# A small read moved up ScalarE's transfer queue, and four bias matmuls moved into the leading tile's x product

## The reference, cut to what matters

```python
h  = x @ W.T + b + ((x @ A[slot]) @ B[slot]) * 2.0        # per batch row of 128 tokens: its own adapter
z  = h @ base_w.T + base_b                                # the second layer
r  = h @ A2.T                                             # 64 hidden columns
p  = softmax(h @ router_w.T)                              # 16 experts
topw, topi = top_k(p, 2); topw = topw / (sum(topw) + 1e-6)
out = x + z + 0.5 * einsum(combine(topw, topi), r, experts)
```

## Time and profile before

| | us |
|---|---|
| runs shown: median of 3 (lowest, highest) | 102.35 (102.18, 102.44) |
| the profiled execution | 102.43 |
| its span in the profile | 100.0 |
| TensorE busy | 96.1 |
| VectorE, ScalarE, GpSimd busy | 66.5, 41.4, 22.3 |
| mean DMA rate over the span | 169 GB/s |

### The profile page before, as it was taken

How to read it: one execution, slowest core, us unless ns; L and a number is a source line. 1 busy time by engine, 2 the same in 40 slices (tenths; PEclk the granted TensorE clock), 3 DMA queues, 4 the chain that set the end, 5 groups by cost and what they waited for, 6 DMA issues and landing times.

```text
span 100.0 us, 1809 instructions
## 1 busy us (share of the span) xinstructions
PE 96.1 (96%) x572; PEld 87.1 (87%) x572; DVE 66.5 (67%) x184; ACT 41.4 (41%) x101; POOL 22.3 (22%) x34
## 2 busy tenths in 40 slices
PE   6899999999999999999999999999999999999990
PEld 6798999999999999998898899878777877878980
DVE  5639997998384884999978567357949275572101
ACT  1705545968778446656531610461334022040000
POOL 4100003234999974208213000000000000000000
PEclk9999999999999999999999999999999999999999
DMA  2999569999958446291970928216228164020211
GB/s 34 370 366 375 179 128 370 290 410 436 328 111 161 158 133 154 61 214 33 239 236 11 253 76 206 108 33 193 99 86 248 29 195 120 0 105 0 105 52 52
DMA packets 8154, 16.90 MB, mean 169 GB/s; under 512 B 1539, under 2 KB 3971, under 8 KB 8018
## 3 DMA queue, kind: packets, MB, share of 16 engines
q1 hardware_dynamic: 7474, 16.41, 53.8%
q10 hardware_dynamic: 640, 0.40, 1.3%
q0 software_dynamic: 32, 0.00, 0.0%
HBM read 13.28 MB, written 2.16 MB: 154 GB/s over the span
## 4 chain that ended last, share of the span: by engine, by line
PE 89%; DMA 6%; DVE 1%; SPq 1%; issue 0%
PE pair L815 86%; DMA w_raw_all<-w_cat 6%; PE pair L957 1%; PE pair L959 1%; PE pair L977 1%; SPq L267 1%; DVE w_hi_all L614 0%; DVE xn L809 0%; PE pair L934 0%; PE pair L947 0%; PE pair L936 0%; PE pair L926 0%
## 5 line engine op out<-in xcount | busy, mean ns | idle before, releaser
L815 PE MATMUL pair<-e_hi,w_hi_all 128*128 128x512 f32 (+1 forms) x72 | 27.1, 376 | 0.0
L815 PE MATMUL pair<-e_hi,w_lo_all 128*128 128x512 f32 (+1 forms) x72 | 26.7, 370 | 0.0
L815 PE MATMUL pair<-e_lo,w_hi_all 128*128 128x512 f32 (+1 forms) x72 | 26.6, 370 | 0.0
L530 ACT ACTIVATE w_hi_all<-exp_raw_all 128x512 fp32r<-128x512 f32 x16 | 9.7, 630 | 15.3 <-DVE exp_raw_all L750 15.3
L815 PEld LDWEIGHTS pair<-e_hi,w_lo_all 128*128 128x128 f32 x72 | 13.5, 188 | 2.5
L815 PEld LDWEIGHTS pair<-e_hi,w_hi_all 128*128 128x128 f32 x72 | 13.5, 188 | 2.5
L815 PEld LDWEIGHTS pair<-e_lo,w_hi_all 128*128 128x128 f32 x72 | 13.6, 189 | 2.0
L757 DVE TENSOR_TENSOR w_lo_all<-exp_raw_all,w_hi_all 128x512 fp32r<-128x512 f32 x16 | 10.4, 689 | 4.5 <-ACT w_hi_all L530 3.9
L750 DVE TENSOR_TENSOR exp_raw_all<-w_raw_all 128x512 f32<-128x512 f32 x16 | 11.4, 753 | 0.0
L764 DVE TENSOR_TENSOR xn<-pair,xn 128x512 f32<-128x512 f32 x7 | 4.8, 690 | 8.9 <-PE pair L815 8.9
L815 PE MATMUL pair<-p_hi,x_hi 128*128 128x304 f32 x32 | 9.9, 310 | 0.0
(11 more groups left out here) (107 smaller groups left out, 162.5 us busy)
## 6 DMA issues: line engine op xcount, KB each, us to landing
w_raw_all<-spill SPq DMA_DIRECT2D x16, 256.0 KB, 4.0
exp_raw_all<-experts SPq DMA_DIRECT2D x4, 512.0 KB, 8.6
xn<-x_n SPq DMA_DIRECT2D x4, 512.0 KB, 7.2
out<-xn SPq DMA_DIRECT2D x7, 256.0 KB, 2.0
w_raw_all<-w_cat SPq DMA_DIRECT2D x3, 552.0 KB, 6.8
xt_raw<-x_t SPq DMA_DIRECT2D x2, 512.0 KB, 6.7
xt_raw<-x_t SPq DMA_DIRECT2D x1, 1024.0 KB, 12.6
c_stack<-c_hi SPq DMA_DIRECT2D x7, 74.0 KB, 3.8
```

The lines of the kernel that those rows point to most:

```text
L530: nc.scalar.activation(gt_hi[:, t % 2, js, :], g[:, js, :], ACT.Copy).then_inc(gh_done, 1)
L815: return nc.tensor.matmul(out_ap, lhs, rhs, start=first, stop=last)
```

## The change

On ScalarE's queue the probe goes out between the left and the right piece of the leading block. On TensorE the four bias matmuls go ahead of the last k of x_other(0), instead of behind it.

```diff
@@ ScalarE @@
-            for n, cols in enumerate((W_LEFT, W_RIGHT)):
-                act.dma_start(w_raw[:, 0, cols], w_cat[0, :, cols]).then_inc(in_w_side[n], 16)
+            act.dma_start(w_raw[:, 0, W_LEFT], w_cat[0, :, W_LEFT]).then_inc(in_w_side[0], 16)
             act.dma_start(probe[:, :, :], w_cat[1:KC, 0:P:8, 0:R].rearrange("k p n -> p k n")).then_inc(in_probe, 16)
+            act.dma_start(w_raw[:, 0, W_RIGHT], w_cat[0, :, W_RIGHT]).then_inc(in_w_side[1], 16)
@@ TensorE @@
             def x_other(t):
                 out_cols, cols = other_half[t % 2]
-                x_side(t, out_cols, cols).then_inc(pe_x, 1)
-
-            def x_side(t, out_cols, cols):
+
+                x_side(t, out_cols, cols, bias_within=t == 0).then_inc(pe_x, 1)
+
+            def x_side(t, out_cols, cols, bias_within=False):
                 par = t % 2
                 x_h, x_l = x_his[t % XB], x_los[t % XB]
                 for k in range(KC):
+                    if k == KC - 1 and bias_within:
+                        bias()
                     if t == 0 and k == 0:
                         pe.wait_ge(pl_done, KC)
...
             x_first(0)
             x_other(0)
-            bias()
             lora_first_transpose()
```

## The result

The changed kernel is slower: 104.94 us median of 6 runs (104.59 to 106.36) against 102.39 (102.06 to 103.25), ratio 1.0241 with an interval of 1.0205 to 1.0276. I had forecast 102.20 and a range up to 103.0. The profiled execution took 105.26, its span is 103.5. Some executions of nearly every kernel here are longer than its others by one per cent or more; the medians keep them, the ratios and intervals leave them out, so a median can lie high beside its ratio.

What follows compares the result with a forecast made beforehand. The bound was taken as the moment the k = 1 block can be multiplied, plus fixed TensorE work and holes. From the 102.35 median, 0.15 off for the bias edit and zero for the queue's edit gave 102.20 us, range 101.85 to 103.0.

Steps and rivals of the forecast that it cites:

- The bound: Whole kernel: time is when the k = 1 block can be multiplied, plus fixed TensorE work, plus holes.
- The bias edit: TensorE in x_other(0): bias sums done 0.42 us earlier, no wait for bp_lo, gain 0.15 us.
- the hole of 0.15: TensorE idle 0.15 us ahead of L934's weight load at 27.06, given to L683's bias_rows; the bias edit closes it.
- The queue's edit: ScalarE's queue: right piece issued 0.45 us later, covered on every path; the sum taken as zero.
- The covers: Lateness of the right piece that costs nothing: up to 0.54 us on ScalarE, 0.9 on TensorE's right rows.
- Rival 2: ScalarE's queue: right piece waits behind the probe's 48 straggling reads, L419 1.95 us late, time 103.6; chance 0.20.
- Rival 1: Ahead of k = 1: earlier probe makes that block land sooner, at most 0.30 us gained, time 101.90; chance 0.30.
- argument from bytes: DMA by 5.50 us: 1185 KB moved, more than both first blocks, so a straggling part, not bandwidth, set k = 1's landing.
- both holes: TensorE idle 0.30 us ahead of k = 1 at 8.12 and 0.15 ahead of L934; both closed would give 101.90.

Runs made afterwards that it cites:

- the last two versions: Kernel before plus the bias edit, probe last: one with table reads behind block 1's casts, 102.22 us (ratio 0.9991); one with block 1 in two transfers, 102.68 (0.998).
- the run in halves: Kernel before plus the bias edit, probe last, block 1 read in two transfers of 552 columns: 102.68 us, ratio 0.998.

## Why the prediction was wrong, point by point

- **The bound, right.** The time is the moment at which block 1 can be multiplied plus fixed work. The + 2.29 is the + 2.43 there less the hole closed. It isn't always block 1's landing that sets this moment: in the profiles without the probe, with the right piece on SyncE's queue and of the last two versions, the chain has TensorE running from the leading block into block 1 without a wait (see the last section).
- **The bias edit, right, and to size in the trace.** L541's idle time went from 0.72 to 0.30 and L683's from 1.27 to 0.84, 0.42 and 0.43, as worked out; the bias sums didn't wait, and the hole of 0.15 is gone in every profile with the edit. In the runs alone it stays at the edge of what they resolve (0.996, up to 0.9997).
- **The queue's edit, wrong.** The step that failed is "I take zero for the sum, since the only thing the rows price directly, the 0.45 of issue, is covered on every path". The covers were there, and a little larger than listed: where the piece was 3.17 late, L427 was 2.43 late and TensorE's right rows 2.00, so 0.74 was covered on ScalarE (0.54 listed) and 1.17 on TensorE (0.9 listed). But 3.17 stood in the place of 0.45. I had priced the issue and left out what the moved transfer meets at the DMA engines: beside SyncE's reads it takes 5.93 us, without them 2.96.
- **The row was there, and I read it wrongly.** The earlier trace rows gave 5.2 to the probe in third place. I took it as a property of the probe ("something holds back part of it"). 1.67 + 5.2 is 6.9, near block 1's 7.53, and in the runs whatever was issued beside block 1 on the other queue landed about with it. The edit put a needed transfer into that place.
- **Rival 2, right in its course, wrong in its cause and price.** The wait ahead of L419, then the table reads, then L427, and ScalarE's queue deciding over TensorE's own end: each step was seen. But I let the piece land with the probe at 6.4; it landed with block 1 at 7.6, and each time after it is 1.0 to 1.2 later than I said (the reads' end 9.95 for 8.97, block 1 10.55 for 9.53 at the latest). That is 1.0 of the 1.3 between my 103.6 and the measured 104.9. It wasn't the small reads either: one does as much harm as 48. The chance of 0.20 was given to a mechanism that isn't there.
- **Rival 1 fell.** Probe 0.48 earlier, block 1 landed at 1.66 + 5.7 = 7.4 instead of 7.53, no more than runs differ. And the run in halves shows that even at 6.6 the gain isn't got. Its argument from bytes was weak too: the 1185 KB were set against the leading block and block 1, but blocks 2 and 3 had been issued by 3.04, and no view tells whose bytes had moved.
- The Trainium skill, "DMA: Bandwidth & Descriptors", which I held to speak for rival 2 by its ring order, has the fitting sentence elsewhere. Its section "Issuing engines are not separate DMA queues" says that transfers started by different engines run on the same 16 DMA engines and interleave. The runs agree: 2.96 us without block 1 beside it, 5.93 with. Its section on queues and rings says that each DMA engine takes turns between its queues by packets. The landings in step with block 1 (5.9 beside 5.7, 6.6 beside 6.5) agree with turns of some kind, though no view shows single turns or what one of them holds.

## What to carry to other kernels

A transfer's place is not only its issue time: ask which transfers of the other queue are at the DMA engines with it, and when those land. Here a small needed piece did no harm on the queue ahead of the big read, or issued before it; an unneeded read belongs last. When a row shows a slow transfer, ask whether the slowness is its own or its place's before moving anything into that place.

## What the runs showed that I had not expected

**Not by bytes.** A piece of 128 KB needed as long as the block of 552 KB beside it; sharing by bytes would have had it out after some 256 KB. Even half of that piece, and the 3 KB of the probe, needed about as long.

**Block 1 lands fast when it is issued late.** 3.4 us after issue when held back to 4.65, 5.6 to 6.5 when issued whole at 1.66. Why it takes so long in the crowd is still open.

**TensorE's clock after the long wait.** With the right piece in short rows TensorE sat idle 3.38 us ahead of 9.91. Stretches of that kernel (stretch, length, the engines, granted clock, DMA share, GB/s):

```profile
6.84:9.91 3.07, 0.00 (x1) 0.03 (x1) 0.11 (x1) 0.42 (x1) 0.00 (x0) 1.00 0.99 382
9.91:10.60 0.69, 0.69 (x4) 0.69 (x5) 0.69 (x2) 0.00 (x0) 0.00 (x0) 0.87 0.98 321
10.60:14.10 3.50, 3.50 (x17) 3.50 (x16) 2.35 (x5) 2.37 (x6) 0.00 (x0) 0.54 0.78 191
14.10:16.00 1.90, 1.90 (x16) 1.90 (x15) 1.87 (x4) 0.96 (x2) 0.00 (x0) 1.00 0.85 207
```

The granted clock went to the lower level (1.2 GHz) shortly after the wait, from about 10.7 to 14.1, and back while TensorE was busy: 17 matmuls in 3.50 us, where 16 took 1.90 after it. In the changed kernel the wait of 1.60 us had no such consequence.

**The leading block's rate differs between executions.** In some profiles its rows of two start 0.49 apart for a while (in the last version above until about 5.8; with the right piece on SyncE's queue for nearly the whole block), in others 0.27 from early on, after the same 13 matmuls on zeros. The clock's column says 1.00 for both, but 0.49 is also how far rows of two start apart in the stretch at 0.54 above, so the column and the starts don't agree in the leading block. By the starts this is up to two microseconds (the leading block takes 5.70, from 4.44 to 10.14, with the right piece on SyncE's queue, and 3.58, from 4.24 to 7.82, in the kernel before), beyond both holes that I had priced, and it would explain why closing them hardly shows in the runs. That was not tried.
